# Fetching table lanes of four pairs, then of two, in pieces of eight rows (time-warping, recurrence and experts kernel)

## What is computed

```python
D = sqrt(maximum(aa + bb - 2.0 * small @ large.T, 0.0))   # small: 1601 context rows, large: 64 rows of x
R[i, j] = D[i, j] + min(R[i-1, j], R[i, j-1], R[i-1, j-1])
...
expanded = zeros((64, 256)).at[j_idx].add(small[i_idx] * valid)   # along the cheapest path
x = x + expanded
```

## Time and profile before

| | |
|---|---|
| three runs | 1256.58, 1258.32 and 1264.05 us; median 1258.32 us |
| profiled execution | 1258.05 us, its span from first to last instruction 1256.6 us |
| busy over the span | PE 1018.7 us, DVE 703.5 us, ACT 485.3 us, GpSimd 83.6 us |
| distances of the first group | first store issued at 29.69 us, last table transfer at 178.36 us |
| first scan of the first group | 188.74 us |
| first scan of the second group | 416.05 us |
| mean granted TensorE clock | 0.921 |

### The profile page before, as it was taken

The page is one execution under the profiler, slowest core; times in us unless marked ns, Lnnn a source line. Parts: engine busy times, 40 slices in busy tenths (PEclk is TensorE's granted clock), DMA queues, the critical chain, the costliest instruction groups (busy, mean ns, idle before and its releaser), DMA issues. The chain is left out here.

```text
span 1256.6 us, 15701 instructions
## 1 busy us (share of the span) xinstructions
PE 1018.7 (81%) x4832; PEld 618.0 (49%) x4832; DVE 703.5 (56%) x2431; ACT 485.3 (39%) x854; POOL 83.6 (7%) x113
## 2 busy tenths in 40 slices
PE   5876636988662599987889578887899999999998
PEld 2332212333220255543656355545677777777776
DVE  5756729999899677496569602346322222222226
ACT  4855434676763244423322144242122222222221
POOL 1000000000000000000000000000122222222210
PEclk9978968999986799989889699889899999999999
DMA  9999974777986979530000098394010011110105
GB/s 365 262 238 289 212 148 134 178 182 177 192 219 99 311 241 329 177 122 1 0 17 1 8 344 277 126 366 170 22 34 31 32 31 34 34 34 30 30 31 192
DMA packets 117407, 179.76 MB, mean 143 GB/s; under 512 B 7600, under 2 KB 91024, under 8 KB 117072
## 3 DMA queue, kind: packets, MB, share of 16 engines
q1 hardware_dynamic: 113584, 168.54, 46.8%
q0 software_dynamic: 3744, 10.23, 2.5%
HBM read 154.32 MB, written 24.42 MB: 142 GB/s over the span
## 5 line engine op out<-in xcount | busy, mean ns | idle before, releaser
L1629 PE MATMUL bank<-w_up,srcT 128*128 x624 | 197.4, 459 | 0.6 <-ACT srcT L1279 0.6
L905 DVE TENSOR_TENSOR hid<-bank,act_s 128x352 f32<-128x352 f32 x110 | 57.4, 524 | 213.6 <-PE bank L1629 208.5
L1416 PE MATMUL bank<-sq,ones 128*64 128x402 f32 (+1 forms) x512 | 107.5, 543 | 48.8 <-ACT sq L1146 48.8
L1629 PEld LDWEIGHTS bank<-w_up,srcT 128*128 128x128 f32 x624 | 117.8, 189 | 54.9 <-issue 0.8
L1287 ACT ACTIVATE act_s<-bank 128x352 f32<-128x352 f32 x110 | 50.8, 464 | 224.5 <-PE bank L1629 224.5
L1432 PE MATMUL bank<-table,ident 128*128 128x402 f32 x144 | 67.1, 550 | 74.1 <-DVE stays L673 67.2
L1410 PE MATMUL bank<-ctxT,latT 128*64 128x402 f32 (+1 forms) x512 | 108.3, 547 | 19.2 <-DMA ctxT<-ctx_tr_dram 18.4
L1655 PE MATMUL bank<-w_dn,hidT 128*128 (+1 forms) x468 | 114.0, 380 | 0.4 <-DVE y_sb L926 0.4
L1487 PE MATMUL bank<-rows_c,on_path 128*64 128x256 f32 (+1 forms) x832 | 100.5, 394 | 11.5 <-DMA rows_c<-ctx_nat_dram 10.7
L1146 ACT ACTIVATE sq<-ctxT 128x1608 f32<-128x1608 f32 x64 | 97.5, 1526 | 11.9 <-DMA ctxT<-ctx_tr_dram 11.9
L1179 ACT ACTIVATE code<-bank,unpassed 128x402 bf16<-128x402 f32 x72 | 42.4, 593 | 135.6 <-PE bank L1434 135.6
(11 more groups left out here) (255 smaller groups left out, 1448.5 us busy)
## 6 DMA issues: line engine op xcount, KB each, us to landing
rows_c<-ctx_nat_dram SPq DMA_DIRECT2D x32, 896.0 KB
ctxT<-ctx_tr_dram SPq DMA_DIRECT2D x32, 804.0 KB, 10.0
ctxT<-ctx_tr_dram SPq DMA_DIRECT2D x32, 797.0 KB, 10.7
rows_c<-ctx_nat_dram SPq DMA_DIRECT2D x32, 640.0 KB
table<-spaced SPq DMA_DIRECT2D x16, 896.4 KB, 12.2
spaced<-dist SPq DMA_DIRECT2D x128, 101.0 KB, 6.7
w_up<-w_t_dram SPq DMA_DIRECT2D x16, 704.0 KB, 12.2
w_dn<-w_t_dram SPq DMA_DIRECT2D x16, 256.0 KB, 4.8
```

The source lines that it names most:

```text
L905: e.tensor_tensor(hid[i][:, :], psum[2 * i + 1][:, 0:HH], act_s[i][:, :], ALU.mult).then_inc(hid_done, 1)
L1416: last = e.matmul(ps[b * T:(b + 1) * T, 0:nq], ones[:, 0:T], sq[i][:, b, k, 0:nq], start=False, stop=(k == KC - 1))
L1629: last = e.matmul(psum[2 * i + m][:, 0:HH], lhsT, rhs, start=(k == 0), stop=(k == KC - 1))
```

## The change

`load_table` now takes two pairs, `first` and `pair`, and fetches the lanes of all pairs from the one to the other with each transfer. A table `LOADED_WITH` says, by the number of a pair within its group, at which pairs a transfer is issued and from which pair on it fetches: at pair 3 the lanes of pairs 0 to 3 (64 partitions), at pair 5 those of pairs 4 and 5 (32), at 6 and 7 their own (16). Where it is more than one pair, nine transfers are issued, each with eight of the 71 rows of all lanes (the last with seven). Every row still reaches the same place. `table_in` rises by 20 x 16 per group instead of 8 x 16.

```diff
+LOADED_WITH = {3: 0, 5: 4, 6: 6, 7: 7}
+FEW_ROWS = 8
...
-        TABLE_IN = 16 * GTILES
+        TABLE_IN = 16 * sum(1 if pair == first else -(-STEPS // FEW_ROWS) for pair, first in LOADED_WITH.items())
...
-            def load_table(pair):
-                g, part = pair // GTILES, 2 * pair % GB * SEGS
+            def load_table(first, pair):
+
+                g, p0, p1 = pair // GTILES, 2 * first % GB * SEGS, (2 * pair % GB + 2) * SEGS
                 e.wait_ge(cleared, g + 1)
                 for i in range(DISTS):
                     e.wait_ge(dist_out[i], dist_slot_value(QUARTERS * pair + i))
-                e.dma_start(table[g][part:part + 2 * SEGS, 1:SLOTS, :].rearrange("p r c -> p (r c)"),
-                            spaced[part:part + 2 * SEGS, :]).then_inc(table_in, 16)
+                rows = FEW_ROWS if first < pair else STEPS
+                for r0 in range(0, STEPS, rows):
+                    r1 = min(STEPS, r0 + rows)
+                    e.dma_start(table[g][p0:p1, 1 + r0:1 + r1, :].rearrange("p r c -> p (r c)"),
+                                spaced[p0:p1, r0 * W:r1 * W]).then_inc(table_in, 16)
...
-                    if u % QUARTERS == 1 and u % GUNITS > QUARTERS:
-                        load_table(u // QUARTERS - 1)
+                    if u % QUARTERS == 1 and u // QUARTERS % GTILES - 1 in LOADED_WITH:
+                        pair = u // QUARTERS - 1
+                        load_table(pair - pair % GTILES + LOADED_WITH[pair % GTILES], pair)
                 if u % GUNITS == GUNITS - 1:
                     store_distance(u)
-                    load_table(u // QUARTERS)
+                    load_table(u // QUARTERS, u // QUARTERS)
```

## The result

| | before | changed |
|---|---|---|
| median of the timed runs | 1259.34 us (1256.58 to 1264.05, 4 runs) | 1247.35 us (1240.35 to 1251.82, 4 runs) |
| profiled execution, its span | 1258.05 us, 1256.6 us | 1247.96 us, 1246.7 us |
| mean granted TensorE clock | 0.921 | 0.919 |
| first scan of the first group (L696, now L699) | 188.74 us | 168.08 us |
| second group's scan with `start` (L703, now L706) | 416.4 us | 398.9 us |

The ratio is 0.9888, 95% interval 0.9844 to 0.9933: about 14 us faster by the ratio and 12.0 by the two medians (the one of before has a fourth run beside the three known), where 21 were forecast. The direction is right, and the size is at the edge: 1247.35 us is 0.35 above the range's upper end of 1247, and well outside the forecast's own range of 1232 to 1242.

What follows compares the result with a forecast made beforehand. The DMA queue was taken to bound the first group, DVE the second. Queue -21.7, idle queue +1, mixing -1, rounded to -21, took 1258.05 to 1237 us; own range 1232 to 1242, with C and D 1227 to 1247.

Steps and rivals of the forecast that it cites:

- The bound: First group: the DMA queue sets the time until about 167 us, then the tail to the first scan at 188.74.
- The price of one table transfer: Loading one pair's table, 16 lanes of 57 KB rows, costs 7.4 us of the whole queue, at 124 GB/s.
- The block of four: At u=17 nine transfers bring pairs 0 to 3, 3.67 MB at the stores' 243 GB/s: 15.1 us, ends 9.3 and 29.6.
- the sum of the queue: First group's queue work up to the tail: -37.0 + 15.1 + 0.2 = -21.7 us, ends -30.4 and 0.
- The wait behind the block: First group, DVE's write of unit 21 waits 4 us for a store, up to 4 more for the next; handed back.
- rival D: DVE takes over from u=5 to u=17, the block's wait is not handed back: gain 12.7 us, 1245 us; chance 0.15.
- The second group: DVE is the bound there, so less queue work gains nothing; the block costs nothing, up to 2 us if longer.
- The spare of 3 us: Second group, unit 53: slope ready near 339.5 us, DVE takes it at 342.60, so 3 us to spare.
- A: The bytes go no faster: block 29.6 us, first group gains zero, second loses about 14, 1272 us; chance 0.06.
- B: Every transfer has a fixed price in the queue, 12 x 1.9 = 22.8 us: gain gone, 1259 us; chance 0.07.
- C: Small pieces run at the context's rate: block 9.3 us, pairs 4 and 5 4.7, -30.4, 1228 us; chance 0.16.

Runs made afterwards that it cites:

- whole rows: The changed kernel with each block fetched by one transfer of 57 KB rows instead of nine of eight rows: 1245.85 us, ratio to before 0.9864.
- single pieces: Against the kernel before, all eight pairs still loaded apart (16 partitions each), but each cut into nine transfers: 1268.55 us, ratio 1.0038.
- the second group alone: Against the kernel before, the change made only in the second group of eight pairs, the first loading pairs one by one: 1260.04 us, ratio 0.9974.
- by twos: Against the changed kernel, pairs 0 and 1, 2 and 3, 4 and 5 joined, 6 and 7 alone, both groups: 1240.28 us, ratio to before 0.9813.

## Why the prediction was right, and what it missed

**The bound, right.** The queue was what held the first group back. With less in it the first scan came (L699) at 168.1 to 169.3 us over three profiles where about 167 was forecast, the store waits before unit 17 went away, and the block of pairs 4 and 5 went out at 125.14 (124 to 127 forecast). The first group changed alone has all of the gain.

**The price of one table transfer, right.** 7.4 us at 124 GB/s came out of three windows, a share times a length, and with it the sum below comes out. That 16 partitions are what makes it slow the forecast only supposed; whole rows and single pieces show it.

**The block of four, mis-sized.** This is the first step that failed: "I take that: 3.67 / 0.243 = 15.1 us". The block costs 18.1 us, and the one of pairs 4 and 5, at 201 GB/s, 9.1 instead of 7.6. With the measured values the sum of the queue is -37.0 + 18.1 + (9.1 - 7.4) = -17.2 us, and the means of the three profiles differ by 186.8 - 169.1 = 17.7 us at the first group's scan. The nearest row by partitions was the wrong proxy. It was the row of stores, which run in the other direction, in pieces of 808 bytes, and whose share of 0.14 has only two digits (4% either way, not the 20% by which it missed). The Trainium skill ("SBUF — State Buffer", "Door 1: The DMA port swizzle") had 196 GB/s for partitions 0..63, which gave 18.7 us and a sum of about -18; the runs agree with it within 4% (203 GB/s), and also that 32 partitions are about as good as 64 (its 189 against 201 here).

**The wait behind the block, right in kind and short in size.** Forecast were 4 us at unit 21 and up to 4 more; measured 9.58 there and 13.3 us over three waits. (DVE's longest wait for PE, 8.2 us, is not part of it: it ends at 21.11, ahead of every table transfer, and before has one of 7.6 us there. Behind the block it waits for PE 1.54 and 0.62 us.) From the block's first issue (82.88) to the write of unit 21 (107.05) it is 24.2 us, where the forecast had 15.1 + 0.8 + 2.3 = 18.2. 3.0 of the 6.0 more are the longer block. The other 3.0 fit what stood ahead of it, which the forecast left out: the context half issued at 79.28 lands up to 8.6 us after its issues, and from 86 to 88 us the queue still moves 388 GB/s, not the block's 203. Nearly all of the wait is handed back as the forecast said, since the queue stays full meanwhile: on the mean the order behind it came 17.6 us early, and the queue's work up to there had fallen by 37.0 - 18.1 = 18.9 us. So rival D's condition held in part (DVE was busy 34.86 of 38 us before the block, 92%, but beside a full queue and not an idle one) and its price did not come: its scan "later than 172" was not seen.

**The second group, wrong.** "Cost nothing; up to 2 us if the block is longer" is the second step that failed. The unchanged part from scan to scan is 227.3 us in all three profiles of before and 229.5 to 230.4 in the changed kernel's: 2.6 us lost. The landing of the context behind the block is in the view of its issues (301.80, two transfers, the least, the middle and the most in us):

```profile
DMA to landing us min/median/max: 16.0/17.7/19.5
```

In the time of before (20.25 us later at this place, by the issues at 313.47 and 293.22) the squares start at 342.0, where 335.5 was forecast: 6.5 us late. 3.0 of them are the longer block, 0.84 is the store of unit 49, which stands between the two and was left out of the sum. For the other 2.7 no row gives the split; some of it is the context itself, whose second transfer takes 7.1 us from issue to landing in the kernel before, where 6.5 was counted. The spare of 3 us was eaten, and DVE waited 2.59 (2.5 and 1.8 in the other two profiles). Whole rows and the second group alone lose 1.5 from scan to scan with a block of the same lanes.

**What is left of 21.** 17.7 at the first group's scan, less 2.6 in the second group, is 15.1 us at the second group's scan (414.1 less 399.0). The ratios of the timed runs, 0.9888 and 0.9893, make 14.1 and 13.5 us, each with some 5 us either way, and 15 agrees with both. The profiled execution alone gives 10.1, since its last stretch was 7.6 us longer than before's; nothing in the edit touches that stretch, and over the kernels it lies anywhere from 840 to 855. The whole of it, before:

```profile
416.00:1256.60 840.60, 748.70 (x3596) 509.67 (x3596) 381.71 (x1384) 247.00 (x499) 77.36 (x83) 0.94 0.33 111
```

and in the changed kernel:

```profile
398.50:1246.70 848.20, 757.08 (x3596) 513.83 (x3596) 381.81 (x1384) 246.70 (x499) 77.15 (x83) 0.93 0.33 110
```

DVE and ACT do the same work in the same time; the same 3596 matmuls keep PE busy 8.4 us (1.1%) longer, at a mean granted clock of 0.93 instead of 0.94. So the 7.6 us are time of PE. Over the twelve profiles PE's busy time in this stretch runs from 748.7 us (this one of before) to 764.0 (single pieces), and by and large the stretch is longer where it is longer. The clock right behind the scan does not decide it: over the first 24 us it was 0.80 in before and 0.70 in the changed kernel's first profile, but 0.80 again in its second, whose last stretch was 847.4 us all the same.

All three of the changed kernel's last stretches (847.4 to 852.4) are longer than the three of before (840.2 to 845.3). That need not be a consequence of the change. The second group alone has 846.9 and arrives no earlier, and the three profiles of before, 1258.1 to 1258.5 us, are among its shorter executions: the runs of before beside the experiments have medians of 1263.11 and 1265.29 us, and the one beside the last three 1266.59. As an estimate, a span of 1263.9 us (the run of 1265.29) with the second scan at 416.4 or sooner leaves 847.5 us or more. But no profile of such a run of before exists, so this stays open. Open, too, is why by twos is 8.3 us faster than the changed kernel by the medians of the same comparison, where 2 to 4 were expected and its second group's scan is only 2.0 us earlier than the changed kernel's mean; the mean clock of its runs was higher (0.924 against 0.921), so part of it may be the clock.

**The rivals.** A (the bytes go no faster): refuted, the block is 18.1 us and not 29.6. Its threshold of 18 us for the second group fits (a wait of 2.6 us with a block of 18.1, none with blocks of about 9), but nothing between was run. B (a fixed price for each transfer in the queue): refuted by the single pieces. C (the context's rate for small pieces): refuted by the same kernel and by whole rows. D (DVE takes over): 1245 us was the nearest number to the result, for another reason than its own, a mis-sized block, a wait in the second group and a longer last stretch. The forecast's own range ended at 1242; that the median came out as near to the stated upper end as it did is owed to a rival whose mechanism did not happen, and in so far to luck.

## What to carry to other kernels

When a queue is full, price each transfer by share times length over a window and find the one that moves fewer bytes per us than its neighbours: 16 partitions cost all 16 engines 7.4 us for 0.9 MB, whatever the size of the pieces; two of them joined cost about 9 where they had cost 14.8. Join no further than the rate rises: two pairs (32 partitions) gave the rate of four at half the piece (whether eight pairs, 128 partitions, would reach the context's 393 GB/s was not tried), and joining the last two as well brought the first scan another 8.7 us forward (169.3 to 160.6), because a slow transfer no longer stood ahead of the stores that the last load waits for. And before costing a larger transfer at nothing, find out what is queued right behind it and how much spare time that has: here it was 3 us by the forecast's count, and DVE waited 2.6 us beyond it.

## What was unexpected of the hardware

- The rate of a table transfer goes by the number of partitions that it spans, and does not rise from 32 to 64: 124 GB/s with 16 (106 in small pieces, in one window of 4 us), 201 with 32, 203 with 64. The context, with 128, moves at 393. From issue to landing, a lone table transfer is a little slower than its share times length says: issued at 401.88 it lands after 10.3 us, and less the 2.3 us of a lone store that is 8.0 us, or about 115 GB/s (an estimate).
- Nine transfers back to back cost the queue nothing beside one: with 64 more of them per group the first scan stood at 187.2 us, between the 184.3 and 188.7 of before. A lone store's fixed 1.9 us is latency, not occupation. They take SP 4.0 to 5.4 us per nine; that kernel as a whole was 0.4% slower (1.0006 to 1.0071), and neither scan shows where.
- A stretch that no edit touches varied by 5 us between profiles of one kernel and by 14 us over all twelve, as much as the effect under study, while the stretch between the two scans repeated within 1 us for both kernels of which there are three profiles. The loss in the second group could be read only from the latter.
